# The last octet of a four-layer cross-attention kernel: its transposes ahead of a projection, its second product on VectorE

## The reference

```
xn = rmsnorm(x, norm_w)
q = (xn @ wq).reshape(B, T, N_HEADS, HEAD_DIM)
k = (cond @ wk).reshape(B, S, N_KV_HEADS, HEAD_DIM)
v = (cond @ wv).reshape(B, S, N_KV_HEADS, HEAD_DIM)
scores = jnp.einsum('btgrd,bsgd->bgrts', qg, k) * scale
attn = jax.nn.softmax(scores.astype(jnp.float32), axis=-1).astype(q.dtype)
out = jnp.einsum('bgrts,bsgd->btgrd', attn, v).reshape(B, T, N_HEADS * HEAD_DIM)
return residual + out @ wo
```

## Time and profile before

| | us |
|---|---|
| median of 3 runs | 376.83 (376.7 to 376.85) |
| the profiled execution | 375.58 |
| its span, first to last instruction | 373.0 |
| TensorE busy | 355.5 |
| ScalarE busy | 280.2 |
| VectorE busy | 248.2 |
| GpSimd busy | 179.8 |

### The profile page before, as it was taken

The page is one execution under the profiler, slowest core; times in us unless marked ns, Lnnn a source line. Parts: engine busy times, 40 slices in busy tenths (PEclk is TensorE's granted clock), DMA queues, the critical chain, the costliest instruction groups (busy, mean ns, idle before and its releaser), DMA issues.

```text
span 373.0 us, 10546 instructions
## 1 busy us (share of the span) xinstructions
PE 355.5 (95%) x3560; PEld 308.8 (83%) x3560; DVE 248.2 (67%) x1384; ACT 280.2 (75%) x1176; POOL 179.8 (48%) x206
## 2 busy tenths in 40 slices
PE   7797999999999999999999999999999999979985
PEld 6676779889989989888878878888999899857774
DVE  1899773564474474679777777467566866679872
ACT  3998997775575576568899999987658666567892
POOL 2696743452232234356666665333323344356751
PEclk9998999999999999999999999999999999999999
DMA  7943000000000000000000000000000000000000
GB/s 220 410 145 145 0 4 2 2 3 0 3 2 2 1 2 2 3 0 3 3 8 9 9 11 2 3 2 2 2 2 3 3 2 1 2 3 0 3 16 14
DMA packets 4883, 9.71 MB, mean 26 GB/s; under 512 B 608, under 2 KB 3296, under 8 KB 4576
## 3 DMA queue, kind: packets, MB, share of 16 engines
q1 hardware_dynamic: 4400, 8.65, 6.5%
q10 hardware_dynamic: 432, 0.40, 0.4%
HBM read 8.53 MB, written 0.52 MB: 24 GB/s over the span
## 4 chain that ended last, share of the span: by engine, by line
PE 83%; DVE 7%; ACT 6%; DMA 1%; issue 1%; SPq 0%; POOL 0%; DVEq 0%; POOLq 0%
PE pt_ps L832 14%; PE scores_ps L819 9%; PE v_ps L884 9%; PE v_ps L866 8%; PE q_ps L771 7%; PE fill_ps L685 5%; PE fill_ps L686 5%; PE fill_ps L687 5%; ACT probs L474 4%; PE v_ps L854 4%; DVE probs L594 4%; PE scores_ps L802 3%; PE scores_ps L685 3%; PE scores_ps L687 2%; PE scores_ps L686 2%; DMA x<-in_xT 1%
## 5 line engine op out<-in xcount | busy, mean ns | idle before, releaser
L474 ACT ACTIVATE probs<-probs,negmax 128x128 f32<-128x128 f32 x512 | 198.4, 391 | 64.7 <-DVE negmax L594 64.4
L375 POOL TENSOR_TENSOR probs<-probs,inv 128x512 f32<-128x512 f32 x128 | 136.0, 1063 | 177.0 <-DVE inv L601 176.8
L474 ACT ACTIVATION_READ_ACCUMULATOR probs<-probs,negmax 128x1 f32 x512 | 96.8, 189 | 0.0
L594 DVE CUSTOM_DVE_ANT_0 probs<-scores_ps,col_bias 128x128 f32<-128x128 f32 x256 | 58.2, 284 | 39.3 <-PE scores_ps L819 39.3
L832 PE MATMUL pt_ps<-smalls,probs 128*128 128x128 f32 x512 | 69.5, 279 | 0.7 <-DVE probsT L605 0.7
L832 PEld LDWEIGHTS pt_ps<-smalls,probs 128*128 128x128 f32 x512 | 56.4, 142 | 14.7 <-issue 12.8
L605 DVE COPY probsT<-pt_ps 128x512 f32<-128x512 f32 x96 | 62.8, 682 | 2.0 <-PE pt_ps L832 1.8
L594 DVE CUSTOM_DVE_ANT_0 probs<-scores_ps,no_bias,inv_rms 128x128 f32<-128x128 f32 x128 | 36.8, 345 | 12.7 <-PE scores_ps L802 12.7
L594 DVE DVE_READ_ACCUMULATOR2_ANT negmax<- 128x1 f32 x512 | 42.7, 83 | 0.0
L819 PE MATMUL scores_ps<-kT,qT 64*128 64x128 f32 x512 | 37.2, 285 | 0.0
L594 DVE CUSTOM_DVE_ANT_0 probs<-fill_ps,no_bias,inv_rms 128x128 f32<-128x128 f32 x128 | 36.5, 341 | 0.0
(11 more groups left out here) (145 smaller groups left out, 634.4 us busy)
## 6 DMA issues: line engine op xcount, KB each, us to landing
kT<-in_kv_w SPq DMA_DIRECT2D x6, 512.0 KB, 6.8
w_qo<-in_qo_w SPq DMA_DIRECT2D x2, 1024.0 KB, 8.4
v<-in_ctxT SPq DMA_DIRECT2D x4, 256.0 KB, 9.6
v<-in_kv_w SPq DMA_DIRECT2D x2, 512.0 KB, 11.2
outT<-x SPq DMA_DIRECT2D x8, 64.0 KB, 1.6
x<-in_xT SPq DMA_DIRECT2D x1, 384.0 KB, 8.0
oT<-in_narrow_kv ACTq DMA_DIRECT2D x1, 320.0 KB, 4.6
wn<-in_narrow_w SPq DMA_DIRECT2D x2, 64.0 KB, 5.7
```

Of the source, the lines that this page charges most:

```text
L375: nc.gpsimd.tensor_tensor(p4, p4, inv[:, o % 2, side, :].unsqueeze(2).broadcast_to([P, 4, S]), ALU.mult,).then_inc(probs_made[side], 1)
L474: last = nc.scalar.activation(e, e, ACT.Exp, scale=-1.0, bias=negmax[:, o % 2, side, q:q + 1], accum_out=rowsum[:, o % 2, side, q:q + 1])
L594: last = nc.vector.tensor_tensor_reduce(out=probs[:, o % PROBS_RING, side, cols], in0=banks[bank][:, cols], in1=bias, scale=scale, scalar= ...
```

## The change

Four edits, all for octet 63 (`LAST`) or behind it:

- TensorE: the transposes of octet 63 leave half 65 and stand in half 64, behind the weighted values of job 30 and ahead of job 30's projection. The four constant products of half 65, and their wait, are gone.
- GpSimd no longer multiplies the second side of octet 63.
- VectorE does it instead (`normalise_last`), directly behind the inverse of that side's sums. It waits for its own semaphore of that inverse, and for GpSimd's product of the second side of octet 62, since both count on the same semaphore.
- VectorE: from half 64 on the first side's copy of octet o-2 stands first in the half. So the copy of octet 62 stands ahead of the inverse of octet 63's second side, and that of octet 63 ahead of job 30's addition.

```
+LAST = 2 * NJOBS - 1
...
                 if valid(o):
                     normalise(o, 0)
-                    normalise(o, 1)
+                    if o != LAST:
+                        normalise(o, 1)
...
+            def normalise_last():
+
+                dve.wait_ge(inv_made[1], LAST + 1)
+                p4 = probs[:, LAST % PROBS_RING, 1, :].rearrange("p (h k) -> p h k", h=4)
+                dve.wait_ge(probs_made[1], LAST)
+                nc.vector.tensor_tensor(
+                    p4, p4, inv[:, LAST % 2, 1, :].unsqueeze(2).broadcast_to([P, 4, S]), ALU.mult,
+                ).then_inc(probs_made[1], 1)
...
                 scores_first = is_narrow(n) and h == 1 and not is_wide(n - 1)
+                if o > LAST and valid(o - 2):
+                    transposes_out(o - 2, 0)
                 if not scores_first:
                     values_bank_out(n, h)
...
                     inverse_sums(o - 1, 1)
+                    if o - 1 == LAST:
+                        normalise_last()
...
-                if valid(o - 2):
+                if valid(o - 2) and o <= LAST:
                     transposes_out(o - 2, 0)
                     if not scalar_copy(o - 2):
                         transposes_out(o - 2, 1)
...
-                if o >= FIRST_WAIT and valid(o - 2):
+                if o >= FIRST_WAIT and valid(o - 2) and o - 2 != LAST:
                     pe.wait_ge(bank_read[Q0], len(BANK_USES[Q0]))
                     warm_up(4, q_ps)
...
-                if valid(o - 2):
+                if valid(o - 2) and o - 2 != LAST:
                     transpose_probs(o - 2)
...
+                if o - 1 == LAST:
+                    transpose_probs(LAST)
                 if h == 0 and n >= 2:
                     output_projection(n - 2)
```

## The result

| | median us | executions |
|---|---|---|
| kernel before | 376.45 (375.29 to 376.85) | 6 |
| changed kernel | 373.68 (372.85 to 374.53) | 6 |
| ratio | 0.9928, 95% interval 0.991 to 0.9946 | |

The change makes the kernel 2.77 us faster. 1.48 us were forecast, and 373.68 lies under the range of 374.9 to 376.2. The sign was right; the size was about half of what was measured.

A forecast was written before the change was run, and what follows sets the result against it. The prediction took the kernel as bound by TensorE, busy 95% of the span, with one string of waits at the end. Starting job 31's weighted values 1.48 us earlier gave 376.83 - 1.48 = 375.35 us, range 374.9 to 376.2.

The forecast's parts named there:

- The order of the tail: Last 10 us: octet 63's transposes precede job 30's projection, so job 31's weighted values start at 367.22, not 368.70.
- the sum: Tail gain of 1.48 us, between 0.86 and 1.61, taken off the median of 376.83 to give 375.35 us.
- one of the prediction's own signs of being wrong: Times of everything before 360 us shifted, which would mean that it is not the tail that moved.
- The cost of the product: VectorE's product for octet 63's second side: 0.69 us, from a same-size subtraction; upper bound GpSimd's 1.063 us.
- the case in which it costs nothing: VectorE's wait on its own semaphore is free, so its product starts 0.13 us earlier: gain 1.61 us, 375.2 us; 15%.
- The second string: Job 30's projection and addition, behind octet 63's transposes, free v_ps at 367.12, 0.10 us before ScalarE's copy arrives.
- The 2.58 us around the span: Profiled execution's 375.58 us less its span of 373.0, from first to last instruction; kept the same in the forecast.
- the cap: Octet 63's second-side transposes can't start before the first side is through, 365.59 against 365.72: at most 1.61 us gained.
- The clock rival: Without the constant products TensorE's clock falls in the tail: up to 2.9 us slower, say 379 us; 4%.

The follow-up runs named there:

- that of the 1935 us: Changed kernel with four constant products put back between octet 63's transposes and job 30's projection, first timing: 375.83 against 376.11 us, ratio 0.9985.

## Why the prediction was right and wrong

**The order of the tail: right.** Each step came within 0.04 us once the late start is added to the predicted times, 1.24 us at VectorE's copy of octet 61 (362.32 before, 363.56 here): copy of octet 62 363.70 + 1.24 = 364.94 (364.97), product 364.89 + 1.24 = 366.13 (366.13), transposes of the first side 366.39 (366.38), ScalarE's copy 366.36 + 1.24 = 367.60 (367.57), the last weighted values 367.22 + 1.24 = 368.46 (368.42). The tail's gain was 1.53 us where the sum had 1.48. That everything before 360 us was shifted is one of the prediction's own signs of being wrong. It appeared by the early clock of that execution, which the diff doesn't touch.

**The cost of the product: right.** The row of a subtraction of the same shape gave 0.694, measured 0.69 us. The wait on VectorE's own semaphore was 0.03 us as in the earlier trace rows; the case in which it costs nothing didn't come (the Trainium skill, VectorE: DVE Perf Modes, The DRAIN you can't avoid, says that of copies in a row). The start stood behind the inverse's end, not before it.

**The second string: right in kind, tight in size.** It stayed hidden. Its slack was 0.2 us where 0.10 was worked out, shown by putting 0.89 us into it and losing 0.68.

**The step that failed** is in the sum: "the part that moves is a fixed piece of the tail, so I take the same difference off". The 2.58 us around the span were taken for a constant. They contained a fetch of instructions, and with the shorter program of TensorE it was gone: 0.88 us (median of 2.68 before, 1.80 after, in 91 and 21 executions). The rows that could have hinted at it, the transfers behind the end of the span, are not among those that it was worked out from. The sum named the constant products that go and gave them 0.89 us on the path, and nothing for their being fewer instructions. With that term it would have been 1.48 + 0.88 = 2.36, 374.5 us, near the 2.34 of all executions together.

**The rest of the first result, 0.4 us,** is chance. Both of its medians are of six executions that fall into two groups 1.3 to 1.4 us apart, so that each can land anywhere between them: 376.45 and 373.68, where all executions together give 376.34 and 374.00. In the baseline of the prediction it was the same: 376.83 was the median of three executions, and it lies among those of the low group, while the profiled 375.58 is one of the high group. Over all, both kernels are half and half. The range was made from the scatter of those three, 0.15 us; the executions of either kernel scatter over more than 2 us.

**The range** had its low end at the cap plus 0.25 us. The cap on the tail was right, and no bound stood for anything outside the tail.

**The clock rival** had 4% and did not come in the changed kernel: no span over 373.2 in 21 executions. But the reason given against it, that TensorE idles less in the new order, is weak. Taking the same products out of the old order lost the clock in half of the executions, and the new order with still less work in the tail kept it. The trace of before could not tell these apart. The Trainium skill (TensorE: Matmul & The Clock Gate, HAM oscillation — how this bites in real kernels) has gaps between bursts bring the low level. The first of the two kernels agrees in kind, 1.90 and 0.80 us in place of 1.08 and 0.49, though none of its gaps in the tail is longer than 0.9 us; the second does not show it.

## What to carry to other kernels

Ahead of a prediction compare the device time with the span and ask what transfers lie behind the span's end; where an edit adds or takes out instructions, a fetch of instructions can come, go, or meet the last store, for 0.8 to 1.6 us here, whatever the edit does to the path. Look at the granted clock of single executions before three of them are taken for a baseline: a gap early in the program split this kernel into two groups 1.5 us apart. And an order that makes one part of a change 0.3 us dear (a product ahead of a copy that others wait for) can be right once the copy is off the path.

## What the runs showed of the hardware

- A fetch of 0.02 MB on the instruction queue q8 goes with more device time where it comes last: in every trace with one behind the span the time around the span is 2.4 to 2.9 us, in every trace without it, but for that of the 1935 us, 1.8. In the two traces where it came with the last store of 64 KB, the store took 3.2 and 3.0 us, and SyncE waited 2.9 and 2.7 us for it in place of 1.3.
- Removing 4 products of constants (8 matrix-product records) from TensorE's program, near its end or 34 us ahead of it, brought the time around the span to 1.76 to 1.85 us in all 12 and 10 executions, and the fetch is gone from the trace of each. With 16 records more than before, early in the program, it was 1.8 us in five of nine as well: what decides is open.
- The clock falls late: with TensorE idle from 31 to 32, the level was 0.50 from about 35 us in the trace of before and already between 32 and 33 in that of the changed kernel. With TensorE busy for 6.8 of the 9 us from 361 to 370 and no gap over 0.9 us, the level was 0.50 from 370 on in one kernel; in others it fell behind the end of the work.
- TensorE took up transposes 0.14 us after VectorE's copy, a projection 0.04 us after VectorE's copy to oT, and weighted values 0.24 to 0.25 us after ScalarE's copy, in the chains that pass there.
- Two of 220 executions took 884 and 1935 us. In the trace of the second the matrix products themselves were many times longer at a granted clock of 1.00 (those of the transposes 1.02 us in the mean, 0.28 in the changed kernel); the cause is open.
